# Selective-scan block on one core: two 512-column scans joined into one of 1024 columns

## The reference

```python
xz = einsum('ed,bld->bel', in_proj_w, xn)                 # xn: layernorm of x, 256 channels each
def direction(xz, ...):                                   # once forward, once on reversed time
    u = silu(causal_conv(x, conv_w) + conv_b)             # 4 taps
    delta = softplus(dtproj(x_proj(u)) + dt_bias)
    dA  = exp(delta * A)                                  # (b, 256, 512, 16)
    dBx = delta * B * u
    h[t] = dA[t] * h[t-1] + dBx[t]                        # the scan over 512 time steps
    return (sum_n(h * C) + D * u) * silu(z)
out = x + out_proj(forward + backward) + (quantize(xn @ H) @ ternary(weight).T)
```

## Time and profile before

| | |
|---|---|
| median of 3 runs | 820.13 us (819.84 to 820.97) |
| profiled execution, its own time | 819.23 us |
| its span, first to last instruction | 817.4 us |
| DVE busy | 738.9 us, 90% |
| PE busy | 726.9 us, 89% |
| POOL busy | 726.9 us, 89% |
| ACT busy | 715.7 us, 88% |
| 512 scans (L592) | 579.4 us busy, mean 1198 ns |
| 255 products with C (L695, POOL) | 596.0 us busy, mean 2371 ns |
| 504 decays (L407, ACT) | 330.6 us busy, mean 709 ns |
| 1536 transposes into b_ps (L910, PE) | 225.3 us busy, 53.8 us idle before them, mostly released by a scan |

### The profile page before, as it was taken

How to read it: one execution, slowest core, us unless ns; L and a number is a source line. 1 busy time by engine, 2 the same in 40 slices (tenths; PEclk the granted TensorE clock), 3 DMA queues, 4 the chain that set the end, 5 groups by cost and what they waited for, 6 DMA issues and landing times.

```text
span 817.4 us, 11915 instructions
## 1 busy us (share of the span) xinstructions
PE 726.9 (89%) x3921; PEld 371.3 (45%) x3921; DVE 738.9 (90%) x800; ACT 715.7 (88%) x1358; POOL 726.9 (89%) x355
## 2 busy tenths in 40 slices
PE   7857998899998899989999999988999889999995
PEld 5324344353644436344453536445363444535353
DVE  4648898998999999998999989999999989999996
ACT  3489998999989998999989999799989999899880
POOL 0269989898998989899898989989899998989996
PEclk9889999999999999999999999999999999999699
DMA  6638063160815327080541708143180805417000
GB/s 198 150 66 191 0 146 78 65 132 4 198 34 132 65 69 167 4 192 2 137 99 52 146 4 193 40 121 78 61 174 4 188 6 129 95 45 152 1 20 20
DMA packets 55118, 74.81 MB, mean 92 GB/s; under 512 B 6784, under 2 KB 23568, under 8 KB 55056
## 3 DMA queue, kind: packets, MB, share of 16 engines
q1 hardware_dynamic: 54624, 73.79, 38.5%
q10 hardware_dynamic: 432, 0.26, 0.1%
HBM read 62.49 MB, written 11.53 MB: 91 GB/s over the span
## 4 chain that ended last, share of the span: by engine, by line
PE 41%; ACT 22%; DVE 10%; issue 7%; POOL 3%; DVEq 0%; ACTq 0%
ACT da L407 13%; DVE hst L592 9%; PE y L933 8%; PE b_ps L888 7%; PE pb L814 7%; PE b_ps L910 7%; ACT dbx_t L394 5%; PE y L919 3%; PE pb L823 3%; PE pb L835 3%; POOL hst L695 3%; PE pb L830 1%; ACT x_ln L312 1%; ACT t_exp L336 1%; PE pb L843 1%
## 5 line engine op out<-in xcount | busy, mean ns | idle before, releaser
L695 POOL TENSOR_TENSOR hst<-hst,c_rep 128x1024 f32<-128x1024 f32 x255 | 596.0, 2371 | 43.1 <-DVE hst L592 30.9
L592 DVE TENSOR_TENSOR_SCAN hst<-da,b_ps 128x512 f32<-128x512 f32 x512 | 579.4, 1198 | 20.1 <-issue 13.0
L407 ACT ACTIVATE da<-rep,neg_a 128x511 f32<-128x511 f32 x504 | 330.6, 709 | 10.2 <-DVE hst L592 10.0
L910 PE MATMUL b_ps<-ident,dbx_t 128*128 128x128 f32 x1536 | 225.3, 283 | 53.8 <-DVE hst L592 50.8
L394 ACT ACTIVATE dbx_t<-du_t,b_t 128x256 f32<-128x256 f32 x576 | 248.4, 496 | 4.7 <-PE b_ps L910 3.9
L910 PEld LDWEIGHTS b_ps<-ident,dbx_t 128*128 128x128 f32 x1536 | 170.1, 142 | 162.8 <-DVE hst L592 100.2
L933 PE MATMUL y<-hst,sum_sel 128*32 128x512 f32 x1024 | 137.3, 609 | 0.9 <-POOL hst L695 0.9
L814 PE MATMUL pb<-xnt,conv_wt 128*128 128x512 f32 x240 | 110.5, 603 | 10.9 <-ACT du_t L377 10.1
L705 POOL TENSOR_TENSOR dbx_t<-du_t,b_t 128x1024 f32<-128x1024 f32 x48 | 91.7, 1910 | 13.7 <-ACT du_t L377 13.7
L888 PE MATMUL b_ps<-du,spread_sel 32*128 32x512 f32 x256 | 89.2, 669 | 1.8 <-POOL du L760 1.2
L581 DVE TENSOR_TENSOR b_ps<-b_ps,b_rep 128x1024 f32<-128x1024 f32 x64 | 77.8, 1217 | 7.9 <-PE b_ps L888 6.6
(11 more groups left out here) (119 smaller groups left out, 460.4 us busy)
## 6 DMA issues: line engine op xcount, KB each, us to landing
rep<-d_scr SPq DMA_DIRECT2D x128, 256.0 KB, 9.2
c_rep<-bc_scr SPq DMA_DIRECT2D x64, 256.0 KB, 4.9
d_scr<-t_pos SPq DMA_DIRECT2D x16, 512.0 KB, 3.0
b_rep<-bc_scr SPq DMA_DIRECT2D x64, 64.0 KB, 2.2
x_ln<-x SPq DMA_DIRECT2D x8, 256.0 KB, 3.9
x_res<-x SPq DMA_DIRECT2D x8, 256.0 KB, 2.8
out<-x_res SPq DMA_DIRECT2D x8, 256.0 KB, 2.3
rep<-x SPq DMA_DIRECT2D x7, 256.0 KB, 4.4
```

What stands on the lines that cost most here:

```text
L407: nc.scalar.activation(da[s % 2][:, j, 1:L], rep[d][h][:, j, 1:L], ACT.Exp, scale=neg_a[:, d, h, j, q:q + 1]).then_inc(decay_done, 1)
L592: nc.vector.tensor_tensor_scan(hst[s % RING][:, j, :], da[s % 2][:, j, :], b_ps[:, j, :], 0.0, ALU.mult, ALU.add).then_inc(scan_done, 1)
L695: nc.gpsimd.tensor_tensor(hst[s % RING][:, two, :], hst[s % RING][:, two, :], c_rep[d][:, q:q + 1, :].broadcast_to([P, 2, L]), ALU.mult).t ...
L910: ins = tr(b_ps[:, j, P * c:P * (c + 1)], dbx_t[(NX * d + q - 1) % 2][:, c, NJ * h + j, :, :].rearrange("p r e -> p (r e)"), ident[:, :])
```

## The change

The two scans of a pair become one operation over 1024 columns, across two banks of b_ps and two tiles of da and hst, which lie side by side. At the first column of the second tile the decay is zero, so that the state of the first tile is multiplied by zero there and the recurrence starts anew. The operation waits for both tiles' inputs and both decays, and adds 2 to scan_done when it ends.

```diff
@@ def scan(b, d, s, p)
-                for j in (2 * p, 2 * p + 1):
-                    dve.wait_ge(t_filled, NJ * S + j + 1)
-                    dve.wait_ge(decay_done, NJ * S + j + 1)
-                    nc.vector.tensor_tensor_scan(hst[s % RING][:, j, :], da[s % 2][:, j, :], b_ps[:, j, :],
-                                                 0.0, ALU.mult, ALU.add).then_inc(scan_done, 1)
+                dve.wait_ge(t_filled, NJ * S + 2 * p + 2)
+                dve.wait_ge(decay_done, NJ * S + 2 * p + 2)
+                row = lambda t: t[:, 2 * p:2 * p + 2, :].rearrange("p j l -> p (j l)")
+                nc.vector.tensor_tensor_scan(row(hst[s % RING]), row(da[s % 2]), row(b_ps), 0.0, ALU.mult, ALU.add).then_inc(scan_done, 2)
```

## The result

The changed kernel takes 823.88 us in the median of 6 runs (823.52 to 826.3), against 819.99 us for the kernel before in runs on the same chip: a ratio of 1.0045, 95% interval 1.0032 to 1.0059. It is slower by 3.9 us. The forecast was 822.8 in a range of 818.9 to 826.5, slower by 2.7.

A forecast was written before the change was run, and what follows sets the result against it. No engine alone bounds the kernel; waits between engines, paced by GpSimd, do. Six forward units at +0.23 and seven backward at +0.20, less 0.08, give +2.7 us: 822.8 us, range 818.9 to 826.5.

The forecast's parts named there:

- The pacemaker and the chain: GpSimd waits once per unit (one direction of one batch, eight steps) at pair A of step 1; thirteen unit lengths decide.
- the forward unit: One forward direction of a batch: one waiting fill +0.43, five pairs of scans -0.20, together +0.23 us; six such units.
- The saving per pair: Each joined scan of 1024 columns was to take 0.04 us less than two of 512; range 0 to 0.098.
- The burst: TensorE fills both banks after the pair's end instead of one; what stands behind the second fill is 0.43 us later.
- The backward unit: One backward direction: side path +0.70 us, 0.42 absorbed by ScalarE's idle, two pairs -0.08; +0.20 us, seven such units.
- The copies: TensorE's fills by copies of du (steps 0 and 1): 1.18 us after the pair's end, 1.13 at once; charged nothing.
- The start on two banks: Joined scan waits for both banks; up to 0.74 us later in steps 4 and 7, covered by VectorE's idle.
- The clock: Rival: TensorE's granted clock falls within the units, about 3 us each; three falls, some 832; chance 0.08 with other stalls.
- The signs: Expected in the changed profile: scans 2.26 to 2.28 us, fills 1.09, 40 TensorE waits; wrong if TensorE's clock falls.
- faster: Rival: VectorE is the bound, each pair gives 0.04 us, 8.3 us in all, 811.8; chance 0.14 with its mild form.
- no change: Rival: joined scan saves more (0.07 us per pair) or half the burst is hidden; +0.5, 820.6 us; chance 0.25.

The follow-up runs named there:

- the coupled kernels: Kernel before, still two scans per pair, with shared waits and shared release: 827.3 us; shared release only: 826.4 us; shared waits only: 819.9 us.
- the kernel with coupled starts: Kernel before, two scans per pair, but the first waits for both banks and both decays; each releases its own: 819.9 us, ratio 1.0006.
- the kernel with the shortest chain: Changed kernel with pairs B of steps 0, 2 and (backward) 5 split into two scans, transposed B moved from step 3 to 2: 820.9 us.

## Why the prediction was right, step by step

**The pacemaker and the chain** were as described. That GpSimd's wait at pair A of step 1 marks a unit and that six forward and seven backward units carry the change is shown by the windows: 4.0 of 4.4 us. That the forward unit hangs on the transposed B is shown by moving it (-0.89 us), and that the loss lies in the release and not in the start by the coupled kernels.

**The saving per pair**, put at 0.04 us with no row for it, is 0.045. The nearest row (0.035) was a good guide. The 75 ns of the Trainium skill (Vector Engine (DVE) Microarchitecture Reference, Measured stream behaviour on trn2) are not borne out for this scan. Another sentence of the Trainium skill is (Perfetto Trace Analysis, Optimizing Scalar/DVE Operations), that breaking instructions up may finish sooner where the engine isn't saturated but causes bubbles on others: joined, VectorE lost 6 us of busy time and the kernel lost 4, and with the pairs B of steps 0, 2 and 5 split again a forward unit took 0.51 and a backward one 0.27 us less.

**The burst**, +0.43 on the forward chain, measured +0.44 at the transposed B. Together with three savings it made u 0.30 us later; with all five savings the forward unit was to be +0.23, and it is +0.37.

**The backward unit**, +0.20: du_t came +0.69 later, forecast +0.70. ScalarE absorbed more than its idle of 0.42, because back-to-back operations start before the one ahead has ended: three of L394 last 1.29 us, but the decay behind them now starts 1.20 after their start. Of the 0.69, about 0.15 reached the end instead of 0.28. The copies made up for that, so 0.22 came out near 0.20 by two errors of opposite sign.

**The copies**, charged at nothing, were the step mis-sized, and they alone are more than what the sum lacks: it had 6 x 0.23 + 7 x 0.20 = 2.8 us, and 6 x 0.37 + 7 x 0.22 = 3.8 came. The prediction compared 1.18 us from the end of pair B to the end of the second copy before with 1.13 for two copies at once, and left out how long the first takes to start. It starts at 392.23, 0.15 us after the scan's end at 392.08, and both are done at 393.36: 1.28 instead of 1.18. The scan behind times_b starts 0.09 us after it instead of 0.04. Splitting this pair gave back 0.12 and 0.10 us per unit, 6 x 0.12 + 7 x 0.10 = 1.4 us in all. That the forecast still lay within 1.1 us of the result is in part luck: in the backward unit ScalarE hid more than was thought, and the share left over happened to stand in for the copies.

**The start on two banks**, hidden: shown, 0.0 us per unit.

**The clock** was a rival with 3 us per fall. It happened in small: in the profile, the forward units with a fall take 47.97 and 47.93 us instead of 47.81 and the backward ones with a fall 48.54 instead of 48.42, some 0.5 us together. With the transposed B moved, one costs up to 1.3.

The sum with measured terms: 6 x 0.37 + 7 x 0.22 + 0.5 = 4.3 less 0.2 for the first backward unit, which did not lose, gives 4.0 + 0.35 for the start of the program = 4.4 us of span. Of the 0.35, 0.25 stand in GpSimd's first row already (44.41 instead of 44.16), before scans matter.

**The signs** came in part. As said: scans of 2.27 us, fills of 1.09 us after a wait, ScalarE's 0.42 us gone, VectorE's busy share down from 94.5 to 92.9% of the thirteen units, GpSimd's idle there up from 33.4 to 36.9 us, 0.27 a unit. Not as said:

- The pitch was to be about 2.22 us. The prediction's own numbers give 2 x 1.114 - 0.04 = 2.19, and 2.18 to 2.19 came.
- ScalarE's idle before the transposed B was to grow to 1.1 us and is still 0.77. The delay shows one wait earlier: in the same place of its list ScalarE waits 0.65 us for a fill (357.41) where it waited 0.38 (355.35 before).
- TensorE was to wait 40 times for scans. It waits 77 times, 58 before transposes and 19 before copies, which were not to wait at all.
- A fall of the clock between 107 and 730 us was to show the prediction wrong, and there were four. By that sign it failed; but the units without a fall carry the loss, and the falls add 0.5 us to it.

Of the rivals, "faster" fell with the coupled kernels, "no change" with the measured saving and a burst that was not half hidden. What was right in "faster" is that joined scans do shorten the units once no release is held back: 47.30 and 48.15.

## What to carry to other kernels

A joined operation also joins its release: count what now starts late behind it, from the end of the operation to the end of the last consumer's burst, and include the start-up of the first consumer. Where a refill stood on the chain, buffer halves that are refilled while the other half is worked on were worth more (0.43 us) than the fixed cost saved (0.045 us). If an engine waits for a release and something on another engine's chain stands behind that wait in its list, move it ahead of the wait; here that was worth 3.1 to 4.4 us.

## What the runs showed of the hardware

The granted TensorE clock fell to 0.50 for 3.4 us in the middle of full work, from 159.2 to 162.6 us for example, with TensorE busy all of that time by the record (window of all engines in the changed kernel, which takes 3.3 us of them). In the 48.1 us ahead of it, from 111.0 on, the granted clock was 1.00 and TensorE was busy for 40.3:

```profile
159.30:162.60 3.30, 3.30 (x16) 1.51 (x15) 3.30 (x2) 3.30 (x8) 3.30 (x2) 0.50 0.19 66
```

These falls came in kernels that differ by where TensorE idles, 0 to 5 in the thirteen units of one execution. What a fall costs depends on what it hits: nothing in the kernel with coupled starts (three falls, units unchanged), up to 0.2 us in the changed kernel, 0.7 in a backward unit of it with the transposed B moved, 1.3 us in a forward unit of the kernel with the shortest chain. In that kernel's profile the falls account for 4.4 us, and its median is no better than before, though its undisturbed units are the shortest.

From the end of the scan waited for to TensorE's first instruction it took 0.06 us before transposes (356.14 to 356.20 in the changed kernel) and 0.15 us before copies of du (392.08 to 392.23).
